# A modulated four-layer convolution stack: the first convolution issued one sample further ahead, with a third buffer for each half of z

## The reference

```python
def _layer(x, style, w, b, mw, mb, typ):
    s = style @ mw.T + mb
    weight = SCALE * w * s[:, None, :, None]
    demod = lax.rsqrt(jnp.sum(weight * weight, axis=(2, 3)) + EPS)
    weight = weight * demod[:, :, None, None]
    if typ == 'same':
        out = jax.vmap(_conv_same)(x, weight) + b[None, :, None]
    elif typ == 'upsample':
        out = jax.vmap(_conv_up)(x, weight.transpose(0, 2, 1, 3)) + b[None, :, None]
        out = _blur(out, 2.0 * blur_k, (1, 1))
    elif typ == 'downsample':
        xb = _blur(x, blur_k, (2, 2))
        out = jax.vmap(_conv_down)(xb, weight) + b[None, :, None]
    return out
out = x
for i, typ in enumerate(TYPES):       # ('same', 'upsample', 'same', 'downsample')
    out = _layer(out, style, weights[i], biases[i], mod_w[i], mod_b[i], typ)
```

## Time and profile before

| | |
|---|---|
| Runs | 1319.05 us median of 3 (1318.85 to 1319.1) |
| Span of the profiled execution | 1316.0 us |
| Its own time beyond the span | not listed; the runs' median is 3.05 us above the span |
| TensorE | matmuls busy 1294.8 us (98%), weight loads 1077.2 us (82%) |
| VectorE | 1155.7 us (88%) |
| ScalarE | 840.8 us (64%) |
| GpSimd | 353.5 us (27%) |
| Mean granted TensorE clock | 0.994 of full speed |

### The profile page before, as it was taken

The page is one execution under the profiler, slowest core; times in us unless marked ns, Lnnn a source line. Parts: engine busy times, 40 slices in busy tenths (PEclk is TensorE's granted clock), DMA queues, the critical chain, the costliest instruction groups (busy, mean ns, idle before and its releaser), DMA issues.

```text
span 1316.0 us, 20135 instructions
## 1 busy us (share of the span) xinstructions
PE 1294.8 (98%) x6565; PEld 1077.2 (82%) x6565; DVE 1155.7 (88%) x1855; ACT 840.8 (64%) x1528; POOL 353.5 (27%) x632
## 2 busy tenths in 40 slices
PE   7799999999999999999999999999999999999998
PEld 6588888888888888888888888888888888888887
DVE  6898988998989899989889899989888888888885
ACT  5666566666565666666666576666566777777774
POOL 3215212133133121124131321121522253332211
PEclk8899999999999999999999999999999999999999
DMA  9235645446654465554556445565554367665643
GB/s 316 79 96 158 186 143 154 141 144 188 173 151 116 140 183 173 148 172 120 160 179 173 142 122 159 158 181 162 167 139 127 104 150 173 181 181 148 174 123 97
DMA packets 95368, 203.38 MB, mean 155 GB/s; under 512 B 10720, under 2 KB 12256, under 8 KB 95264
## 3 DMA queue, kind: packets, MB, share of 16 engines
q1 hardware_dynamic: 94896, 201.81, 53.4%
q10 hardware_dynamic: 368, 0.28, 0.1%
HBM read 72.39 MB, written 67.24 MB: 106 GB/s over the span
## 4 chain that ended last, share of the span: by engine, by line
PE 95%; DVE 3%; issue 1%; ACT 1%; POOL 0%; DMA 0%; SPq 0%; ACTq 0%; DVEq 0%; POOLq 0%
PE ps L463 93%; PE ps L565 1%; PE ps L395 1%; DVE gf L1035 0%; PE ps L443 0%; DVE gl L1071 0%; DMA gh<-gh 0%; DVE xl L978 0%; DVE vf L1014 0%; DVE vl L1021 0%; DVE gf L1041 0%; DVE vh L1023 0%; DVE zl L984 0%; ACT kp L750 0%; DVE X L993 0%
## 5 line engine op out<-in xcount | busy, mean ns | idle before, releaser
L463 PE MATMUL ps<-zh,gh 128*128 128x512 f32 (+1 forms) x1028 | 408.6, 397 | 5.8 <-DMA gh<-gh 3.7
L463 PE MATMUL ps<-zl,gh 128*128 128x512 f32 (+1 forms) x1028 | 406.4, 395 | 0.0
L721 ACT ACTIVATE zh<-ps,t_bx 128x512 fp32r<-128x512 f32 x256 | 175.5, 685 | 295.7 <-PE ps L463 293.3
L750 ACT ACTIVATE kp<-ps,t_T1s 64x256 f32<-64x256 f32 x512 | 213.2, 464 | 136.2 <-PE ps L463 132.9
L463 PE MATMUL ps<-zh,gl 128*128 128x512 f32 (+1 forms) x1028 | 282.5, 396 | 0.0
L993 DVE SCALAR_TENSOR_TENSOR X<-ps,t_D,X 128x512 f32<-128x512 f32 x255 | 189.8, 744 | 69.9 <-PE ps L463 43.8
L463 PEld LDWEIGHTS ps<-zh,gh 128*128 128x128 f32 x1028 | 194.6, 189 | 53.4 <-issue 5.2
L984 DVE SCALAR_TENSOR_TENSOR zl<-ps,t_bx,zh 128x512 fp32r<-128x512 f32 x256 | 190.5, 744 | 49.3 <-ACT zh L721 45.6
L463 PEld LDWEIGHTS ps<-zl,gh 128*128 128x128 f32 x1028 | 195.0, 190 | 45.2
L463 PEld LDWEIGHTS ps<-zh,gl 128*128 128x128 f32 x1028 | 194.1, 189 | 45.1
L978 DVE SCALAR_TENSOR_TENSOR xl<-X,t_S,xh 128x513 fp32r<-128x513 f32 x256 | 204.4, 818 | 4.5 <-ACT xh L709 2.4
(11 more groups left out here) (204 smaller groups left out, 1546.0 us busy)
## 6 DMA issues: line engine op xcount, KB each, us to landing
out_x<-X SPq DMA_DIRECT2D x255, 256.5 KB, 5.0
X<-out_x SPq DMA_DIRECT2D x96, 513.0 KB, 6.9
gh<-gh SPq DMA_DIRECT2D x127, 240.0 KB, 3.0
gl<-gl SPq DMA_DIRECT2D x127, 240.0 KB, 3.6
X<-x_in SPq DMA_DIRECT2D x32, 513.0 KB, 8.3
pk<-taps_in SPq DMA_DIRECT2D x3, 512.0 KB, 11.9
pk<-pack_in SPq DMA_DIRECT2D x3, 352.0 KB, 11.1
pk<-sets_in SPq DMA_DIRECT2D x4, 256.0 KB, 8.4
```

The costliest lines, as they stand in the source:

```text
L463: return pe.matmul(out_ap, a, b, start=first, stop=last, skip_group_check=True)
L721: act.activation(zh[n % 2][:, ZPAD:ZPAD + M], ps[:, ZP + n % 2, :], IDENT, bias=tab["bx"][:, k, b:b + 1]).then_inc(s["zhi"], 1)
L750: return act.activation(kp[rows, to, i, :], got[of, :, j, :], ACT.Copy, scale=tab["T1s"][of, k, b:b + 1])
```

## The change

TensorE's step n becomes k_products, **conv0(n+2)**, setup and edge work, convg(n), v_products; conv0(2) is issued behind convg(0). `xhi` and `xlo` are made for sample n+4 in step n where they were made for n+3. `zh` and `zl` have three buffers each, n % 3; zhi(n) waits for convg(n-3). PSUM banks stay as they are, two for z. `spread(q)` gets a wait for convg before its first DMA, and GpSimd clears the borders of the two new buffers (four more memsets at its start).

```diff
-        zh = [sb(f"zh{i}", [128, M + 4], F32R) for i in range(2)]
-        zl = [sb(f"zl{i}", [128, M + 4], F32R) for i in range(2)]
+        zh = [sb(f"zh{i}", [128, M + 4], F32R) for i in range(3)]
+        zl = [sb(f"zl{i}", [128, M + 4], F32R) for i in range(3)]
...
             def spread(q):
+                if q:
+                    sp.wait_ge(s["convg"], max(QS * (q - 1) + 1, 3))
...
                 if n == 0:
                     convg(n)
-                elif n + 1 < NN:
-                    conv0(n + 1)
+                if n + 2 < NN:
+                    conv0(n + 2)
...
-                if n >= 2:
-                    act.wait_ge(s["convg"], n - 1)
-                act.activation(zh[n % 2][:, ZPAD:ZPAD + M], ps[:, ZP + n % 2, :], IDENT,
+                if n >= 3:
+                    act.wait_ge(s["convg"], n - 2)
+                act.activation(zh[n % 3][:, ZPAD:ZPAD + M], ps[:, ZP + n % 2, :], IDENT,
...
             xhi(4)
+            xhi(5)
...
-                if n + 3 < NN:
-                    xhi(n + 3)
+                if n + 4 < NN:
+                    xhi(n + 4)
...
-                dve.scalar_tensor_tensor(zl[n % 2][:, ZPAD:ZPAD + M], ps[:, ZP + n % 2, :], tab["bx"][:, k, b:b + 1],
-                                         zh[n % 2][:, ZPAD:ZPAD + M].bitcast(F32), ALU.add, ALU.subtract) \
+                dve.scalar_tensor_tensor(zl[n % 3][:, ZPAD:ZPAD + M], ps[:, ZP + n % 2, :], tab["bx"][:, k, b:b + 1],
+                                         zh[n % 3][:, ZPAD:ZPAD + M].bitcast(F32), ALU.add, ALU.subtract) \
...
             xlo(4)
+            xlo(5)
...
-                if due is None and n + 3 < NN:
-                    xlo(n + 3)
+                if due is None and n + 4 < NN:
+                    xlo(n + 4)
```

More of the change, by code:

```diff
@@ L483, in convg @@
                 q, i, b = n // QS, n % QS, n % 2
-                o, h, l = ps[:, OP + b, :], gh[:, n // 2 % 3, b], gl[:, n // 2 % 3, b]
+                o, h, l, zhn, zln = ps[:, OP + b, :], gh[:, n // 2 % 3, b], gl[:, n // 2 % 3, b], zh[n % 3], zl[n % 3]
                 taps_at = [(2 * j, slice(ZPAD + d, ZPAD + d + M)) for j, d in enumerate((1, 0, -1, -2))]
@@ L491, in convg @@
                             c, to = slice(ZPAD + d + part, ZPAD + d + part + M // 2), ps[:, EP if part else OP + b, part:part + M // 2]
-                            add(to, h[:, 2 * j:2 * j + 2, :], zh[b][:, c], first=(j == 0))
-                            add(to, h[:, 2 * j:2 * j + 2, :], zl[b][:, c])
-                            m = add(to, l[:, 2 * j:2 * j + 2, :], zh[b][:, c], last=(j == 3))
+                            add(to, h[:, 2 * j:2 * j + 2, :], zhn[:, c], first=(j == 0))
+                            add(to, h[:, 2 * j:2 * j + 2, :], zln[:, c])
+                            m = add(to, l[:, 2 * j:2 * j + 2, :], zhn[:, c], last=(j == 3))
                         m.then_inc(s[name], 1)
@@ L504, in convg @@
                 for j, c in taps_at:
-                    add(o, h[:, j:j + 2, :], zh[b][:, c], first=(j == 0))
-                    add(o, h[:, j:j + 2, :], zl[b][:, c])
+                    add(o, h[:, j:j + 2, :], zhn[:, c], first=(j == 0))
+                    add(o, h[:, j:j + 2, :], zln[:, c])
                 if n < 2:
@@ L511, in convg @@
                 for j, c in taps_at:
-                    m = add(o, l[:, j:j + 2, :], zh[b][:, c], last=(j == 6))
+                    m = add(o, l[:, j:j + 2, :], zhn[:, c], last=(j == 6))
                 m.then_inc(s["convg"], 1)
@@ L1250, in _ @@
             sig(pool.memset(warm[:, :], 0.0), "warm")
-            for a in (zh[0], zh[1], zl[0], zl[1]):
+            for a in zh + zl:
                 for cols in (slice(0, ZPAD), slice(ZPAD + M, ZPAD + M + 2)):
```

## The result

| | before | after |
|---|---|---|
| Runs, median (lowest to highest) | 1318.95 us (1317.03 to 1319.1), 4 runs | 1355.07 us (1353.08 to 1355.36), 4 runs |
| Ratio of after to before | | 1.0273, 95% interval 1.0261 to 1.0285 |
| Span of the profiled execution | 1316.0 us | 1353.6 us |

Slower by 36 us: the direction and the range were right, the predicted 1345.7 us was 9.4 us short. By its spans the change costs 37.6 us.

The account below looks back on a forecast made before the run. TensorE, matmuls busy 98% of the span, was taken as the bound. Stalls 19.8, restarts 2.6, a removed stall −0.7, start 3.5 and sample 4's four 1.4 sum to 26.6: 1319.05 becomes 1345.7 us; own range 1333 to 1356, 8-in-10 range 1330 to 1358.

Parts of the forecast that it names:

- The moved wait: TensorE's conv0(n+2) needs zlo(n) to free its PSUM bank, so zlo is due one conv0, 1.40 us, earlier.
- the start: First samples: conv0(3), now ahead of convg(1), waits for xh(3) and xl(3); net cost 3.5 us.
- the start's bounds: 1 us if the FIR runs without GpSimd beside it, 8 us if stops bring some 20 half-speed matmuls; 4.9 taken.
- 26 fours: Four-sample stretches forecast to stall at conv0, at most; each stall could be 0.3 us larger or smaller.
- The price of the longer fours: Fours where VectorE takes longer, mostly through GpSimd, stall conv0 about 0.8 to 2.0 us each; 17.5 us with restarts.
- It just fits: cost 0: In a plain four, VectorE's last zlo ends just in time for the earlier conv0, margin 0.07 us; no cost.
- plain fours stall as well: Rival: shifted GpSimd w3 steps or a 0.2 us release cost about 60 fours 0.15 us each; 1355 us, chance 0.10.
- The release: Time from the end of VectorE's zlo to the TensorE matmul it releases, taken as about 0.05 us.
- The gap for zh: VectorE's only standstill in a plain four, 0.13 us before a zl; gone after the change as zhi comes early.
- Edits without a price: x look-ahead, third z buffers, SyncE's new wait, GpSimd's four memsets and the tail were all said to cost nothing.
- conv0(3)'s stop: TensorE idles 5.5 us near 33 us, before conv0(3), waiting for xh(3) and xl(3).
- Places of the waits: TensorE's waits for zl rise to some 15 to 20 us in some 25 places, each ahead of conv0 behind k_products.

Follow-up runs that it names:

- wait_only: Kernel before, with only the moved wait: from sample 8 on conv0(n) waits for zlo(n-1), not zlo(n-2); 1344.88 us.
- banks_fixed: three_banks, but the last block keeps its old edge steps and the old first step of its stores; 1328.53 us.
- w3_later: Changed kernel with ScalarE's w3hi behind xhi(n+4), so that GpSimd's w3 steps start later; 1343.59 us.
- buf_only: Kernel before with the third zh and zl buffers alone, TensorE's order and x look-ahead as before; 1317.92 us.
- start_old: Changed kernel with conv0(3) kept at its old place behind convg(1) and k_products(1); 1346.82 us.
- three_banks: Changed kernel with a third PSUM bank for z; edge results share one bank and some edge jobs come a step later; 1338.34 us.

## Why the prediction was right, and where it failed

- **The moved wait** was the cause of all but the start, and is shown: wait_only brings 27 us with nothing else changed, and a third bank takes the stalls away (banks_fixed).
- **The number** lies in the forecast's own range (1333 to 1356), but partly by luck: that range was made of the start's bounds and of sizes in 26 fours, and what filled it were 28 plain fours priced at nothing, beside the start.
- **The price of the longer fours** held: 17.5 us forecast with their restarts, 14.6 measured. Reading end of zlo less start of conv0 in the trace of before was enough for this.
- **"It just fits: cost 0"**, of plain fours, failed: 28 plain fours cost 11.4 us. The rival "plain fours stall as well" named both reasons and 1355 us, and had 0.10; it was to come from some 60 fours at 0.15 us and came from 28 at 0.40. The margin of 0.07 us came from two misreadings that cancel. The release is 0.15 us at every conv0 that stalled, and the 0.05 was another place's. The gap for zh was 0.22 us and not 0.13: the row ahead of it gives way after 0.66 us (175.59 to 176.25), and the end of its 0.74 us, 176.34, was taken. The release alone made plain fours 0.2 us longer, but only where that gap is still there (wait_only). In the changed kernel it is the collision that decides: without it plain fours fit (w3_later). The argument against the rival, that the rows repeat to 0.01 us, says only that they repeat while no engine beside them moves, and the change did move ScalarE.
- **"Edits without a price"** was right of the buffers by themselves (buf_only). But ScalarE's freedom, which comes from the earlier conv0 and the buffer together, was priced at nothing and is what moved GpSimd. I had followed the earlier zh, not the earlier w3h. ScalarE's wait with zh moved to kp (132.9 us before, 185.2 after) as said, but mostly to gf and vh, which the forecast did not name; xh has 29.2 us.
- **The start** was mis-sized: 3.5 us forecast, 7.1 measured. conv0(3)'s stop was right (5.3 for 5.5). The second stretch at the lower clock was only in the upper bound of 8 us, and w3l's wait in none. The other kernels with this start have 6.0 to 7.8 us, all over the forecast. start_old shows that all of it hangs on conv0(3).
- **Places of the waits:** 18.1 us lies within the forecast 15 to 20, but in 47 places, not 25: the plain fours again.
- **Left open:** of the 1.2 us in the last samples, 0.7 goes with one more stall of conv0 for zl (at 1326.3 us), and 0.5, behind convg(254), has no explanation. Open is also how much of the third bank's 3.9 us the moved edge jobs cost, and how far the second stretch at the lower clock would go if its stops were each a little shorter.

## What to carry to other kernels

In this kernel more look-ahead on TensorE needed a PSUM bank more, for the result that is in flight longer, and buffers in SBUF were no substitute: ask which reader of the bank the earlier matmul now has to wait for, and compare the end of that reader's whole ordered stretch with the new deadline, four by four. A margin the size of one release is none, and it must be read again with the other engines where the change puts them: an engine that is set free moves the collisions of its followers. Whoever moves a step ahead in an in-order engine's list has to look at its input at every place where it will stand, the heads of the stretches above all.

## What the runs showed of the hardware

- A VectorE step on SBUF that starts while GpSimd runs w3h or w3l is held until about GpSimd's end: 0.85 us for 0.42 where GpSimd's step ended 0.56 us into it (34 of 34 in the changed kernel), and xl 1.12 us for 0.74. One that started 0.05 or 0.18 us ahead of GpSimd's was not held (26 before, 32 in w3_later, all 0.42 or 0.43 us). xnew and zl, which read PSUM, were not held inside a GpSimd step either (0.73 to 0.75 us in every one). It doesn't hold for every GpSimd instruction: three xl steps inside its ye and three inside its en took their 0.74 us.
- GpSimd's w3h and w3l are held in turn: 0.74 us alone, and an end 0.59 to 0.61 us behind the vl, vh or xl in which they start. GpSimd's spans are rough in a profile in general; these repeat to 0.01 us.
- From the end of VectorE's zl to the matmul that waits for it: 0.15 us at all 47 stalls of conv0 in the changed kernel (338.55 to 338.70), and at all 25 in wait_only. At the head of a convg it was 0.06 us (one place before, four in banks_fixed).
- A stop of 0.16 us of idle time costs a plain four 0.4 us in all. The matmul ahead started at 338.26, and at the pace before it (0.12 us) conv0 would have started at 338.38; it starts at 338.70, 0.32 us late, and the next matmuls lose 0.08 us more (0.70 for 0.63). The matmuls' modelled ends hide the rest.
- Stops of 1.50, 1.36 and 2.17 us, at 56.84, 62.66 and 66.02, were followed by a stretch at 1.2 GHz, as one of 5.28 us was by itself; two of 0.99 and 1.15 us, at 57.56 and 59.90 before, were not.
- The landing of two 240 KB transfers took 11.3 us in three_banks, right behind eight stores of 256.5 KB, and 7.6 us in banks_fixed, with four stores in front of them and 6.5 us between; the median of all such transfers in the changed kernel is 2.9 us.
